# A new order for ScalarE's work in the rounds of a sliding-window attention

## The reference, cut to what matters

```
q = h @ Wq.T + bq        # 64 heads of 64
k = h @ Wk.T + bk        # 8 heads; each serves 8 query heads
v = h @ Wv.T + bv
s = q k^T * 64**-0.5     # masked: causal, and at most 128 keys back
p = softmax([s, sink])   # the sink's share is dropped after the sum
x = x + ga * ((p v) @ Wo.T + bo)
```

## Time and profile before

| | before |
|---|---|
| median of 3 runs | 3884.02 us (3883.19 to 3885.53) |
| profiled execution, its own time | 3884.02 us |
| span of its profile | 3882.2 us |
| busy: PE / DVE / ACT / POOL | 91% / 79% / 58% / 37% |
| mean granted TensorE clock | 0.944 of full |

### The profile page before, as it was taken

One profiled execution on the slowest core, in us unless ns is written; L12 is line 12 of the kernel. 1 busy time (PEld: TensorE's weight loads), 2 busy tenths in 40 slices (PEclk: granted clock), 3 DMA queues, 4 the chain that ended last, 5 costly groups with the idle time before them and its releaser, 6 DMA issues.

```text
span 3882.2 us, 93870 instructions
## 1 busy us (share of the span) xinstructions
PE 3539.9 (91%) x32894; PEld 2472.2 (64%) x32894; DVE 3062.9 (79%) x11272; ACT 2233.1 (58%) x6991; POOL 1441.5 (37%) x1741
## 2 busy tenths in 40 slices
PE   7999999999999989999989969989878999899955
PEld 6888888888888866666644433335555666555532
DVE  7888888888888866677779967768876777788771
ACT  5888888888888842257654434433333222477611
POOL 2554554554455410045448855520000000222117
PEclk9999999999999989989999989999987999799958
DMA  3000000000000013210000000000000000000023
GB/s 130 3 3 3 3 3 2 3 3 3 3 3 3 3 45 91 72 67 2 2 1 1 0 11 0 1 1 1 1 1 34 1 1 1 33 2 2 23 60 49
DMA packets 30897, 64.58 MB, mean 17 GB/s; under 512 B 3424, under 2 KB 19808, under 8 KB 29152
## 3 DMA queue, kind: packets, MB, share of 16 engines
q1 hardware_dynamic: 24288, 52.29, 3.9%
q0 software_dynamic: 6144, 6.30, 1.0%
HBM read 49.93 MB, written 8.65 MB: 15 GB/s over the span
## 4 chain that ended last, share of the span: by engine, by line
PE 67%; DVE 19%; issue 5%; ACT 5%; POOL 2%; DMA 1%; DVEq 0%; POOLq 0%; ACTq 0%; SPq 0%
PE ps L176 8%; PE ps L537 7%; PE ps L497 7%; PE ps L521 6%; PE ps L473 5%; PE ps L1674 3%; PE ps L1643 3%; PE ps L1645 3%; PE ps L2285 3%; PE ps L2298 3%; DVE gbbc L2337 2%; PE ps L1014 2%; DVE gbbc L2326 2%; DVE gbbc L2332 2%; PE ps L978 2%
## 5 line engine op out<-in xcount | busy, mean ns | idle before, releaser
L736 ACT ACTIVATE T<-T 128x128 f32<-128x128 f32 x1024 | 396.9, 397 | 11.9 <-DVE T L663 11.9
L736 ACT ACTIVATE W<-T 128x128 f32<-128x128 f32 x1024 | 397.2, 399 | 1.3 <-DVE T L663 1.3
L643 DVE CUSTOM_DVE_ANT_0 T<-ps,C 128x128 f32<-128x128 f32 x1536 | 381.4, 286 | 0.0
L653 DVE COPY_PREDICATED W<-gbbc,ps 128x512 f32<-128x512 int32 x512 | 342.8, 722 | 3.2 <-PE ps L176 2.6
L497 PE MATMUL ps<-T 64*64 64x192 f32 (+2 forms) x8192 | 317.0, 291 | 16.9 <-DVE T L643 16.9
L537 PE MATMUL ps<-W,gbbc 64*64 64x128 f32 (+1 forms) x6912 | 319.6, 310 | 2.1 <-DVE W L653 1.2
L497 PEld LDWEIGHTS ps<-T 64*64 64x64 f32 x8192 | 255.6, 133 | 95.4 <-issue 60.6
L176 PE MATMUL ps<-C,T 128*128 128x128 f32 (+1 forms) x1620 | 262.3, 299 | 50.7 <-DVE T L307 19.0
L1241 POOL TENSOR_TENSOR QK<-T,QK 128x512 fp32r<-128x512 f32 x128 | 161.9, 1274 | 381.1 <-ACT T L1201 263.8
L537 PEld LDWEIGHTS ps<-W,gbbc 64*64 64x64 f32 x6912 | 280.4, 132 | 28.3 <-PE ps L537 23.1
L827 POOL TENSOR_TENSOR W<-W,T 128x512 f32<-128x512 f32 x256 | 260.8, 1040 | 77.3 <-DVE T L670 77.3
(11 more groups left out here) (420 smaller groups left out, 8822.6 us busy)
## 6 DMA issues: line engine op xcount, KB each, us to landing
T<-crow_dram SPq DMA_DIRECT2D x128, 128.0 KB, 3.0
W<-in_l1f_dram SPq DMA_DIRECT2D x1, 6152.0 KB, 18.1
W<-in_l0a_dram SPq DMA_DIRECT2D x1, 5172.5 KB, 25.5
W<-in_l2f_dram SPq DMA_DIRECT2D x1, 3160.0 KB, 10.5
W<-in_l3f_dram SPq DMA_DIRECT2D x1, 3076.0 KB, 10.0
W<-in_sm_dram SPq DMA_DIRECT2D x1, 2729.0 KB, 8.9
W<-in_l0f_dram SPq DMA_DIRECT2D x1, 2256.0 KB, 30.3
X<-in_x_dram SPq DMA_DIRECT2D x1, 2048.0 KB, 7.6
```

What stands on the lines that cost most here:

```text
L643: done(e.tensor_tensor_reduce(sm[:, at:at + 128], src, m, 1.0, -3.0e38, ALU.add, ALU.max, mx[:, col:col + 1]), s["masked"], x == (3 if ban ...
L653: e.copy_predicated(a.PT[t % 2][:, 512 + 512 * j:1024 + 512 * j].rearrange("p (h w) -> p h w", h=4), is_.unsqueeze(1).broadcast_to([P, 4, ...
L736: done(e.activation(a.Pr[i % 4][:, at:at + w_], a.Sm[i % 2][:, at:at + w_], ACT.Exp, bias=a.ngs[i % 4][:, c:c + 1], scale=a.scale, accum_o ...
```

## The change

It reorders ScalarE's instructions in a round. The second `outputs` comes after the first three exponentials of group n and not before all of them. The first `turned` comes ahead of `project` and not behind it, and both come after six exponentials and not after four. All waits keep to the instructions that they belong to. No other engine's program changes.

```diff
         if leaving is not None:
             outputs(2 * leaving)
+        if n is not None:
+            begin(2 * n)
+            weights(2 * n, 0, 3)
+        if leaving is not None:
             outputs(2 * leaving + 1)
         if n is not None:
-            begin(2 * n)
-            weights(2 * n, 0, 4)
+            weights(2 * n, 3, 6)
+        if turning is not None:
+            turned(2 * turning)
         if ahead is not None:
             project(ahead)
-        if turning is not None:
-            turned(2 * turning)
         if n is not None:
-            weights(2 * n, 4, 8)
+            weights(2 * n, 6, 8)
             sinks(2 * n)
```

## The result

The changed kernel takes 3936.54 us (median of 4 runs, 3925.64 to 3940.66), the kernel before 3883.61 us (median of 4). The ratio is 1.0134, with a 95% interval of 1.0111 to 1.0156: slower by some 50 us (the interval is 43 to 61 us). The forecast was 3931, 47 us more than before. The profiled execution took 3932.3 us with a span of 3930.5, which is 48.3 us more than the span before.

A forecast was written before the change was run, and what follows sets the result against it. TensorE was taken to bound the first attention stage. Steady rounds 44.7, border rounds 1.5 and round 0 0.4 us sum to 46.6, added to 3884.0 for 3931 us; range 3910 to 3946 (8 in 10).

The forecast's parts named there:

- TensorE bounds the stage, and only its waits count: First attention stage: TensorE busy 82.68 of 83.54 us a batch, so time changes only where TensorE starts or stops waiting.
- q0 0.94 later, the k/v load 0.51 late: Steady round: ScalarE's q0 activations start at 708.82, not 707.88, so TensorE's k/v load starts at 709.71, not 709.20.
- 0.10 comes back, 0.41 lost: Steady round on TensorE: loads following the k/v load come 0.44 us after it, not 0.54, so 0.41 of 0.51 is lost.
- The bound from below (0.14): Least loss per steady round: `out` runs 0.37 us past the k/v load's start, so a costless load leaves 0.14 us.
- the prediction's own range: Loss of 0.33 to 0.51 us a steady round, with border rounds, giving 3921 to 3942 us.
- The second `outputs` is no cost: ScalarE's second output copy ends at 707.305, letting TensorE load `out` at 707.355, 0.115 us before it is wanted.
- Border rounds lose 0.10: In 15 batch-border rounds the k/v load is 0.20 us late, less 0.10 recovered: 0.10 us lost each.
- Round 0 loses 0.4: The stage's first round was counted as losing 0.4 us once.
- The sum of 46.6: Total added time: 109 steady rounds at 0.41, 15 border rounds at 0.10 and round 0 at 0.4 make 46.6 us.
- The clock stays at 1.00: New short TensorE gaps do not lower its clock; the rival that it falls (4%) gave 3970 us.
- What the profile after should show: Forecast signs: k/v projection waits about 0.4 us a round, 45 us in sum; none at `out`; batch about 86.5 us.
- The faster rival: ScalarE's earlier exponentials put VectorE ahead, removing 15 border waits of 0.86 us: 13 us saved, 3871 us; chance 4%.

The follow-up runs named there:

- dose experiments: Kernel before, both `outputs` first, with five, six or eight exponentials, then `turned`, ahead of `project`: 3893.48, 3924.99 and 4023.20 us.
- split_only: Kernel before with only the second `outputs` moved behind three exponentials, `project` still after four and ahead of `turned`: 3887.74 us, ratio 1.0012.
- q0_after_6: Kernel before with both `outputs` kept together, then six exponentials, `turned` and `project`: 3924.99 us, ratio 1.0096.
- q0_after_5: Kernel before with both `outputs` kept together, then five exponentials, `turned` and `project`: 3893.48 us, ratio 1.0023.
- defer_before: Kernel before with VectorE's border work (addition to x, both statistics) put behind the masks of the next group's first unit: 3877.71 us, ratio 0.9977.
- defer_split: Kernel before with VectorE's border work cut in two: addition and first statistics ahead of the reciprocal, second ahead of the k/v move: 3873.06 us, ratio 0.9954.
- after_again: The changed kernel run once more, unedited, beside the other kernels: 3931.71 us, ratio 1.0127 against the kernel before.

## Why the prediction was right

- *TensorE bounds the stage, and only its waits count*: shown. ScalarE's idle time before `outputs` grew to 1.42 us (forecast: about 1.5) and nothing came of it.
- *q0 0.94 later, the k/v load 0.51 late*: measured 0.49. The new order lasts as added up from the old rows; the hand-over of 0.05 us from round 1 held to the hundredth (724.17 to 724.22). Of the 0.94, 0.43 were room (709.20 less the end of the q0 activations at 708.72 and less the hand-over).
- *0.10 comes back, 0.41 lost*: 0.38 lost, and by the dose experiments 0.10 to 0.11 comes back at each lateness tested. The bound from below (0.14) was far off. The 0.33 that the prediction's own range starts from has no row behind it: by its bound of 0.14 the range would have reached down to 3899. What of the load is hidden is not the whole time that `out` is still in the array.
- *The second `outputs` is no cost*: right, by split_only. The margin was put too high, at 0.115 us where it was 0.06, because the hand-over to `out` took 0.12 and not the 0.05 of q0.
- *Border rounds lose 0.10*: right. The load there starts 422.51 − 417.09 = 5.42 us behind ScalarE's first copy, before 407.19 − 401.94 = 5.25: 0.17 late, forecast 0.20. What that costs shows beside q0_after_6, which loses nothing in a border round: 86.35 − 86.27 = 0.08. The batch grew by 2.81, that is 2.73 in seven steady rounds (0.39 each; the rounds' 10.66 and 10.28 are rounded) and 0.08 at the border. Forecast for the batch was 86.5, measured 86.35.

```profile
417.09 0.60 ACT L749 ACTIVATE T<-ps 128x512 f32<-128x512 f32 x1 [1.64 <-PE ps L537]
```

```profile
422.51 0.30 PEld L464 LDWEIGHTS ps<-HT,W 128*128 128x128 f32 x2 [0.21 <-ACT T L729]
```

- *Round 0 loses 0.4*: not seen, and not tested either. q0's four matmul records took 2.07 us there at the lower clock, where before they took 1.13, so that ScalarE waited 1.31 us for q0 even behind six exponentials. It hardly counts.
- *The sum of 46.6*: the changed order itself accounts for 3.0 + 39.3 + 1.5 = 43.8 us in the profile. The other 4.5 of the span's 48.3 are the start of the stage at the lower clock, and the rest of the program. The medians are 53 us apart, 9 more than the 43.8 (which the interval of 43 to 61 still holds), and nothing in the rounds accounts for these. So the mechanism was forecast within 3 us (46.6 for 43.8), and that 3931 and 3936.5 lie as close as they do is in part chance.
- *The clock stays at 1.00*: right, 1.00 in the batch, with TensorE busy for 98% by its records.
- *What the profile after should show*: wrong in one point. I expected 0.4 us of matmul idleness in each round and 45 us in the list of waits. The matmul rows leave only 724.22 − (722.21 + 1.89) = 0.12 us, too little for the list: k and v stand there among TensorE's matmul waits only for the first rounds. The loss shows in the weight loads (63 us waited in 126 rounds, 0.5 each, of which 0.38 is lost), in the distance between rounds and in VectorE's wait.
- *The faster rival* put the borders' worth at 13 us and made it hang on ScalarE. The runs show that ScalarE has no hold on them, and VectorE's own order has. They were worth 16 us.

## What to carry to other kernels

Before moving work on an engine that is idle part of the time, take the end of the wait that anchors it, add up the new order from there, and compare each output with the moment at which the busiest engine loads for it: here 0.43 us of room, and 0.10 more that cost nothing: the `turned` and one more exponential fitted (q0_after_5), the `turned` and two did not. A move out of a shared PSUM bank is such a deadline, and belongs ahead of work that has time. The gain was not on ScalarE at all but in VectorE's order at the batch borders, where the only waits of the bounding engine stood.

## What the runs showed of the hardware

- TensorE's load of k or v, behind `out` in this order, cost nothing for the first 0.10 to 0.11 us that it was late, and from there on its whole lateness (0.00, 0.38 and 1.15 us lost at 0.11, 0.48 and 1.25 late). The load of `out` fits the same line (0.20 lost at 0.31 late, one point).
- Idle time between matmul records was too small by 0.20 to 0.26 us here. At 1.25 us of lateness the record showed 0.89 idle and 1.15 was lost; in the changed kernel 0.12 against 0.38; at the border 0.86, and taking it away gave 1.09; in defer_before 0.33, where the batch is 0.53 above that of defer_split. The loss is read from the period of a round or a batch.
- From the end of a ScalarE instruction to the start of the TensorE load that waited for it were 0.05 us behind the q0 activations (128x256) and 0.12 us behind the copy of the outputs (128x512). Why they differ is open.
- The whole program varies outside this stage: from the first turn behind it to the end of the span were 2485.6 us before, 2486.3 after, 2480.6 in after_again, 2493.7 in split_only and 2494.8 in q0_after_6, with code that is the same. Why is open. A change of some us can be told by its batch and not by one time.
